# A language-model tower on one core: weights fetched in the first stage, decay attention's folding moved into its ramp, routing weights spread in pairs

## What is computed

```
h = tok(x)                                  # two gathered halves of a row, each projected and gated
h = h + attn(layernorm(h))                  # one head of 64
h = h + block(layernorm(h))                 # rms norm, rotary attention (4 heads), then 8 experts, top 2
    hh = silu(flat @ w1[e].T) * (flat @ w3[e].T);  out += weights[:, e] * (hh @ w2[e].T)
h = h + decay(layernorm(h))                 # causal filter of 5 taps, layer norm, attention of 8 heads
    p_ = softmax(scores);  dist = sqrt((total - cumsum(p_)) * pos);  scores *= exp(-softplus(gamma) * dist)
h = h + mlp(layernorm(h))                   # routed: the 63 best tokens of a sequence go through gelu MLP
```

## Time and profile before

| | us |
|---|---|
| median of three runs | 2688.34 |
| lowest and highest | 2672.03, 2693.78 |
| profiled execution, its own time | 2694.7 |
| its span in the profile | 2692.7 |
| PE busy | 2431.4 (90%) |
| DVE busy | 1908.5 (71%) |
| ACT busy | 1464.7 (54%) |
| POOL busy | 1203.3 (45%) |
| bytes moved by DMA, mean rate | 21.31 MB, 8 GB/s |

### The profile page before, as it was taken

How to read it: one execution, slowest core, us unless ns; L and a number is a source line. 1 busy time by engine, 2 the same in 40 slices (tenths; PEclk the granted TensorE clock), 3 DMA queues, 4 the chain that set the end, 5 groups by cost and what they waited for, 6 DMA issues and landing times. The chain is left out here.

```text
span 2692.7 us, 57001 instructions
## 1 busy us (share of the span) xinstructions
PE 2431.4 (90%) x20912; PEld 1545.5 (57%) x20912; DVE 1908.5 (71%) x4056; ACT 1464.7 (54%) x2886; POOL 1203.3 (45%) x1544
## 2 busy tenths in 40 slices
PE   6999859999959999999999659999999999999485
PEld 5988736777742222222222147777777777776364
DVE  4589637777746666666666558999899999986524
ACT  1234326666643333333333237888888898886332
POOL 6356114444420000000000037888788888875361
PEclk9999759999979999999999868999899999996677
DMA  2111000000000000000000000000000000000003
GB/s 46 24 36 39 8 8 2 2 2 2 2 19 1 1 1 1 1 1 1 1 1 1 23 1 2 2 2 2 2 2 2 2 2 2 2 2 2 5 1 63
DMA packets 31477, 21.31 MB, mean 8 GB/s; under 512 B 24537, under 2 KB 28761, under 8 KB 31220
## 3 DMA queue, kind: packets, MB, share of 16 engines
q0 software_dynamic: 6144, 9.84, 1.6%
q1 hardware_dynamic: 25076, 8.03, 1.3%
HBM read 13.66 MB, written 4.19 MB: 7 GB/s over the span
## 5 line engine op out<-in xcount | busy, mean ns | idle before, releaser
L1123 ACT ACTIVATE act<-c_h 128x512 f32<-128x512 f32 x352 | 210.2, 597 | 407.1 <-PE c_h L1054 407.1
L1210 DVE TENSOR_TENSOR hid<-c_wb,prod 128x512 f32<-128x512 f32 x352 | 243.0, 690 | 241.6 <-PE c_wb L1063 233.0
L1054 PE MATMUL c_h<-flatT,e_w 64*128 64x512 f32 x704 | 398.5, 646 | 10.5 <-DVE owner L1200 10.4
L1055 PE MATMUL c_h<-flatT,e_w 64*128 64x512 f32 x704 | 398.5, 646 | 0.0
L1026 POOL TENSOR_TENSOR H<-H,c_turned 128x256 f32<-128x256 f32 x32 | 23.4, 731 | 691.1 <-ACT c_turned L1117 691.1
L1362 POOL TENSOR_TENSOR d_decay<-d_later,d_posg 128x768 f32<-128x768 f32 x128 | 233.4, 1824 | 48.4 <-DVE d_later L1752 48.3
L1218 DVE TENSOR_TENSOR prod<-c_h,act 128x512 f32<-128x512 f32 x352 | 239.4, 680 | 0.2
L1752 DVE TENSOR_TENSOR_SCAN d_later<-d_cont,d_S 128x384 f32<-128x384 f32 x256 | 229.3, 937 | 1.6 <-ACT d_S L1669 1.6
L1054 PEld LDWEIGHTS c_h<-flatT,e_w 64*128 64x128 f32 x704 | 104.4, 186 | 181.1 <-ACT act L1123 133.4
L1073 PE MATMUL c_out<-hid,e_w 128*64 128x512 f32 x704 | 206.7, 617 | 0.1
L1063 PEld LDWEIGHTS c_wb<-wT,owner 24*128 24x128 bf16 x352 | 31.9, 91 | 267.9 <-issue 169.8
(11 more groups left out here) (348 smaller groups left out, 6060.4 us busy)
## 6 DMA issues: line engine op xcount, KB each, us to landing
out_h<-g_Y SPq DMA_DIRECT2D x8, 512.0 KB, 4.0
rows<-in_table,idx POOLq DMA_INDIRECT x128
e_w<-in_e_w SPq DMA_DIRECT2D x1, 704.0 KB
e_w<-in_e_w SPq DMA_DIRECT2D x1, 352.0 KB
d_conv<-in_d_conv SPq DMA_DIRECT2D x1, 320.0 KB
d_wqk<-in_d_wqk SPq DMA_DIRECT2D x1, 256.0 KB
d_pos<-in_d_pos SPq DMA_DIRECT2D x1, 192.0 KB
d_cont<-in_d_cont SPq DMA_DIRECT2D x1, 192.0 KB
```

The lines of the kernel that those rows point to most:

```text
L1054: nc.tensor.matmul(b1[u][:], w13[0:D, cols], flatT[0:D, x], start=True, stop=True).then_inc(h1_made, 1)
L1055: nc.tensor.matmul(b3[u][:], w13[D:P, cols], flatT[D:P, x], start=True, stop=True).then_inc(h3_made, 1)
L1123: nc.scalar.activation(act1[q % 2][:], b1[q % 2][:], ACT.Silu).then_inc(activated, 1)
L1210: nc.vector.tensor_tensor(hid[q % KEEP_HID][:], bw[u][:], prod[u][:], ALU.mult).then_inc(weighted, 1)
```

## The change

Four edits go together.

1. All weight tiles are allocated once (`early_constants`), and SP issues the 51 loads of the four later stages right behind the 11 of the embedding stage (`load_early`), with one semaphore a stage. The later stages have no SP program of their own for loads; DVE, PE and ACT wait for the same counts as before (the expert stage for 6 in place of 5, because `owner` is fetched twice).
2. The decay stage clears four small tiles, and its loop starts at once. The folding is cut up: convolution at K = -14, projections (with the constants of v) at -11, decay rates and mask at -8, positions in four slices at -7 to -4, the carried bias at -1. Each user waits for the semaphore of its part: PE at its first filter, its first projection and its first scores, ACT at its first copy of v, POOL at its first use of the positions. The instruction mix is the same.
3. The routing weights stand twice in `wts`, now bf16 and padded to 2 x 32 columns, so that the turned `wT` has 24 rows at partitions 0 and 24 at partition 32, and so has `owner`. `spread` runs at even steps only and makes the weights of two chunks, one from each strip, into the two banks. Its wait is for both banks (`weighted >= q`). The turning is a bf16 matmul with an identity in place of an fp32 transpose; the spare columns are cleared by POOL.
4. Routing runs on eighths of the sequences (`QUARTERS = NG // 4`) with one step at every chunk (`PACE` 1, was 3); the first eighth is ahead of everything.

```diff
 phase_embed_attend, sync
+                load_early(sp, dram, T, early)
 phase_block_attention
-            @block.sync
-            def _(sp):
-                for dst, name in ((wq, "f_wq"), (wk, "f_wk"), (wkp, "f_wkp"), (wv, "f_wv"), (wo, "f_wo"),
-                                  (ln1, "f_ln1"), (ln2, "f_ln2"), (router, "router")):
-                    for half in range(2):
-                        sp.dma_start(dst[half * D:(half + 1) * D, :], dram[name]).then_inc(loaded, 16)
...
 phase_experts
-    QUARTERS = NG // 8
+    QUARTERS = NG // 4
...
-    ROUTE, PACE = 25, 3
+    ROUTE, PACE = 25, 1
...
-        wts = m.sb("wts", [P, NB, PARTS, NE])
+        wts = m.sb("wts", [P, NB, 2, STRIP], BF16)
...
+                pool.memset(wts[:, :, :, SPAN:], 0.0).then_inc(spare, 1)
...
-                        last = nc.tensor.transpose(bt[0:PARTS * NE, b * P:(b + 1) * P],
-                                                   wts[:, n * GB + b].rearrange("p k e -> p (k e)"), ident[:])
+                        last = nc.tensor.matmul(bt[0:2 * STRIP, b * P:(b + 1) * P],
+                                                wts[:, n * GB + b].rearrange("p k e -> p (k e)"), ident_b[:],
+                                                start=True, stop=True)
...
                 def spread(q):
-                    n, c, u = q // NCH, q % NCH, q % 2
-                    if c == 0:
-                        pe.wait_ge(wT_kept, n + 1)
+                    pe.wait_ge(wT_kept, (q + 1) // NCH + 1)
                     if q >= 2:
-                        pe.wait_ge(weighted, q - 1)
-                    nc.tensor.matmul(bw[u][:], owner[:, c * P:(c + 1) * P], wT[n % 2][:], start=True, stop=True)\
-                        .then_inc(wb_made, 1)
+                        pe.wait_ge(weighted, q)
+                    for side in range(2):
+                        n, c = (q + side) // NCH, (q + side) % NCH
+                        rows = slice(side * STRIP, side * STRIP + SPAN)
+                        nc.tensor.matmul(bw[side][:], owner[rows, c * P:(c + 1) * P], wT[n % 2][rows, :],
+                                         start=True, stop=True).then_inc(wb_made, 1)
...
-                    if t < LAST:
+                    if t < LAST and t % 2 == 0:
                         spread(t)
...
+                nc.vector.tensor_copy(ident_b[:], ident[:]).then_inc(ready, 1)
                 nc.vector.tensor_scalar(w13[:], w13[:], ln2[:, 0:1], None, ALU.mult).then_inc(ready, 1)
-                nc.vector.tensor_copy(owner[:], owner_f[:]).then_inc(ready, 1)
+                for side in range(2):
+                    rows = slice(side * STRIP, side * STRIP + SPAN)
+                    nc.vector.tensor_copy(owner[rows, :], owner_f[rows, :]).then_inc(ready, 1)
 phase_decay_attention
+        PREPARE_CONV, PREPARE_PROJ, PREPARE_SOFT = FIRST_STEP + 2, FIRST_STEP + 5, FIRST_STEP + 8
...
+                        if m + 1 == 0:
+                            pe.wait_ge(carried, 1)
+                            nc.tensor.matmul(bT[:, 0:D], bv_wide[:], wout[:, 0:D], start=True, stop=True)\
+                                .then_inc(folded, 1)
+                            pe.wait_ge(proj_ready, PROJ_READY)
...
+                def spread_positions(pair):
+                    heads = slice(2 * pair, 2 * pair + 2)
+                    nc.vector.tensor_tensor(posg[:, heads], pos[:, None, :].to_broadcast([P, 2, SEG]),
+                                            over(gam[:, heads], SEG), ALU.mult).then_inc(soft_ready, 1)
...
                 for K in range(FIRST, LAST + 1):
                     m, j = K // PAIRS, K % PAIRS
+                    if K == PREPARE_CONV:
+                        prepare_convolution()
+                    if K == PREPARE_PROJ:
+                        prepare_projections()
+                    if K == PREPARE_SOFT:
+                        prepare_softmax()
+                    if PREPARE_SOFT < K <= PREPARE_SOFT + PAIRS:
+                        spread_positions(K - PREPARE_SOFT - 1)
+                    if K == -1:
+                        carry_bias()
+                        dve.wait_ge(soft_ready, SOFT_READY)
...
+def load_early(sp, dram, T, loaded):
+    for name in ("f_wq", "f_wk", "f_wkp", "f_wv", "f_wo", "f_ln1", "f_ln2", "router"):
+        for half in range(2):
+            sp.dma_start(T[name][half * D:(half + 1) * D, :], dram[name]).then_inc(loaded["block"], 16)
+    for name in ("rope_q", "cos_k", "sin_k", "hide"):
+        sp.dma_start(T[name][:], dram[name]).then_inc(loaded["block"], 16)
+    for name in ("rank", "e_ln2", "e_w13"):
+        sp.dma_start(T[name][:], dram[name]).then_inc(loaded["experts"], 16)
...
```

More of the change, by code:

```diff
@@ L970, in phase_experts @@
     PARTS = 3
+    SPAN = PARTS * NE
+    STRIP = 32
     NG = NB // GB
@@ L1731, in _ @@
-                for u in range(2):
-                    nc.vector.memset(later[u][:, 0:1], 0.0).then_inc(chain, 1)
-                for u in range(KEEP_V):
-                    nc.vector.memset(v[u][:, :, :, HD:HD + 1], 1.0).then_inc(chain, 1)
-                    nc.vector.memset(v[u][:, :, :, HD + 1:], 0.0).then_inc(chain, 1)
-                steps[0] += 2 + 2 * KEEP_V
-                dve.wait_ge(chain, steps[0])
-                nc.vector.memset(xT[:, :, 0:PADT], 0.0).then_inc(ready, 1)
-                nc.vector.memset(rstd[:], 0.0).then_inc(ready, 1)
@@ new lines, in load_early @@
+def load_early(sp, dram, T, loaded):
[6 more added lines that the diff above has]
+        sp.dma_start(T[name][:], dram[name]).then_inc(loaded["experts"], 16)
+    for side in range(2):
+        rows = slice(side * 32, side * 32 + dram["owner"].shape[0])
+        sp.dma_start(T["owner"][rows, :], dram["owner"]).then_inc(loaded["experts"], 16)
+    sp.dma_start(T["e_w2"][:], dram["e_w2"].rearrange("(c p) n -> p c n", p=P)).then_inc(loaded["experts"], 16)
+    for name in ("d_wqk", "d_wv", "d_wout", "d_conv", "d_beta", "d_convb", "d_lnw", "d_lnb", "d_bqk", "d_bv", "d_outb",
+                 "d_gam", "d_pos", "d_cont", "d_hide", "d_notfirst", "d_half"):
+        sp.dma_start(T[name][:], dram[name]).then_inc(loaded["decay"], 16)
+    sp.dma_start(T["d_diag"][:], dram["ident"]).then_inc(loaded["decay"], 16)
+    for half in range(2):
+        sp.dma_start(T["g_w1"][half * D:(half + 1) * D, :], dram["g_w1"]).then_inc(loaded["mlp"], 16)
+    for name in ("g_b1", "g_b2", "g_wr", "g_br"):
+        sp.dma_start(T[name][:], dram[name]).then_inc(loaded["mlp"], 16)
+    sp.dma_start(T["g_w2"][:], dram["g_w2"].rearrange("(c p) n -> p c n", p=P)).then_inc(loaded["mlp"], 16)
@@ L2124, in tower @@
         ident = m.sb("ident", [P, P])
+        T = early_constants(m, dram)
         const_loaded = m.sem("const_loaded")
+        early = {stage: m.sem(f"early_{stage}") for stage in ("block", "experts", "decay", "mlp")}
         with nc.Block() as block:
```

259 lines of the change are left out of this document (133 added, 126 removed).

## The result

The changed kernel takes 2565.74 us (median of 4, 2562.83 to 2578.17), the one before, measured beside it, 2689.55 us (2672.03 to 2693.78): a ratio of 0.957, 95% interval 0.952 to 0.962. Medians and ratios in this document leave out executions that took over 1.5% longer than the fastest of the same kernel. The profiled execution has a span of 2561.1 us against 2692.7. Direction and mechanism came as forecast; the gain is larger than the sum of -95.3 us.

The account below looks back on a forecast made before the run. PE was taken to bound the expert stage, no single engine the decay stage, with idle stretches between stages. Terms -53 - 3 - 6.7 - 14.0 - 5.4 - 15.2 + 2 = -95.3 us gave 2593 us, range 2570 to 2619.

Parts of the forecast that it names:

- Pairs, -53: Expert stage: two spreading matmuls run side by side in one slot, 176 x 0.30 = 53 us less, PE still the bound.
- (a): Rival, expert stage: the spreading pair does not overlap, -17.6 in place of -53, 2628 us; chance 0.10.
- (d): Rival, expert stage: PE stalls at each pair waiting for DVE's hid, slower than before, 2725 us at 0.75 us a stall; chance 0.02.
- stage of about 656 us: Sign, expert stage: PE at 99% or more of a stage of this length, period of two chunks 3.44 us.
- Turning, -3: Expert stage: 32 times four fp32 transposes become bf16 matmuls, 7 us in all, cut to 3 for weight loads between them.
- Routing head, -6.7: Start of expert stage: load wait -5.0, extra casts +0.9, routing steps on half the elements -2.6 us.
- Block loads, -14.0: Start of block stage: DVE's wait for small DMAs, 357.0 to 371.10 us, goes whole, 14.0 us.
- Decay, -15.2: Decay stage start: no load wait, folding partly hidden in the ramp, 15.2 us less; bounds -10.1 and -30.3.
- Last stage, -5.4: Start of last stage: DVE's load wait of 5.40 us goes.
- Embedding, +2: Embedding stage: early loads contend with row gathers for the DMA engines, 2 us more; bounds 0 and 14.7 us.
- rival (c): Decay stage: PE's mean clock differs by execution, 2583 or 2603 us; inside the forecast's range, no chance of its own.
- (b): Rival: gathers collide with loads in the embedding stage (+12.7) and the decay ramp hides no folding (+5.1), 2611 us; chance 0.09.

Follow-up runs that it names:

- x_old_experts: Changed kernel with the expert stage of before (single spreading, fp32 turning, routing in quarters), weights still loaded early: 2666.5 us, expert stage 734.8 us.
- x_late_loads: Changed kernel with each later stage's weights again fetched at that stage's own start: 2632.6 us median, ratio 0.974 to the kernel before.
- x_after_64: Changed kernel with the spreading pair on rows 0 to 63 and 64 to 127, eight turning matmuls a group: 2540.5 us median, ratio 0.941 to the kernel before.
- x_before_64: Kernel before with its single spreading matmul widened by rows of zeros to 64 rows: 2619.0 us, expert stage 679.1 us.
- the first four experiments: Changed kernel with late loads (2632.6 us), folding ahead of the ramp (2583.8 to 2654.7), old expert stage (2666.5), or both pair matmuls on the same rows (2607.5).
- x_64_back: Changed kernel with pairs on 64-row strips and output matmuls ahead of the products at odd visits: 2564.3 us median beside 2585.2 of the changed kernel.
- r_after: Changed kernel profiled once more, unchanged, beside the kernel before on the same chip: span 2583.4 us.

## Why the prediction was right, and where it was not

- **Pairs, -53.** Right in the mechanism: they start together, DVE's wait is hidden, PE stays the bound; rivals (a) and (d) are refuted by the pair's one slot of 0.31 us and by 623 busy us in 627. The size was off: the stage came out at 657.9 us, where the sum gives 739.7 - 62.7 = 677.0. (The "stage of about 656 us" among the signs is the window of 713 us less 57, not this stage; that it is near 657.9 is chance.) The failed step is the slot of a pair costed alone ("176 x 0.30"): the prediction saw the 0.10 us for a change of kind, but put it only at the spreading matmul itself. The product passes on both sides of a visit pay it too, 0.53 against 0.43 us. Where the visit goes and products meet products, 0.20 more is saved, 66 times by count of the order: 13.2 us.
- **Turning, -3.** It takes 0.32 us (0.54 before), not 0.45: 32 x 0.22 = 7.0 us. I had taken weight loads to stand between the four; the slot leaves no room for them. These two make 17 of the 19 us by which the stage beat its forecast; 2 are not assigned.
- **Routing head, -6.7.** As measured. Each part fits: casts and folding end at 754.07, 5.3 us after the start, and a routing step lasts 0.29 us. The loads' share is 4.9 by the stage with all else old (x_old_experts); late in the new stage they cost 7.8 (x_late_loads).
- **Block loads, -14.0.** The wait of 14.09 us is gone; the stage gained 16.7, and 15.9 by x_late_loads. The prediction counted the wait alone. What the other 2 to 3 us are no run tells apart: they are within the spread of one profile (412.8 to 416.9 us with the same code), though the means of eight and four profiles differ by 16.5; and the record shows 50 us of the lower clock in that stage after, 73 before.
- **Decay, -15.2.** -15.6 at the first scores. Late loads bring them back by 11.4, folding ahead of the ramp by 5.9 us: both parts near the 10.1 and 5.1 of the working. From the first scores to the stage's end the same code took 909.9 to 924.4 us in seven profiles, the code of before 915.0 to 921.4 in three: no effect there beside the clock. Against the second and third profile of the old code (58.1 and 58.2) the scores came 16.8 and 16.9 us earlier.
- **Last stage, -5.4.** The second table load comes 30.0 us after the start, 35.6 before: -5.5. But the stage is 8.0 us longer, so 13.5 were lost behind that point. It goes with the clock: with the same code the stage lasts 184.7 us with 89 us of lower clock in it, 189 with 97 and 200 with 118. The profile after has 21.6 us more of the lower level there than the one before, half of which is 10.8; the other 2.7 stay open. Step wrong: none in the term; that the saving would survive in one execution's stage length.
- **Embedding, +2.** PE's waits for rows, which answer to the earlier trace rows, and PE at the same place of both kernels later, after and then before:

```profile
33.92 0.49 PE L249 MATMUL a_rows_T<-ident,rows 128*75 128x128 f32 x1 [2.35 <-DMA rows<-in_table,idx]
45.51 0.63 PE L249 MATMUL a_rows_T<-ident,rows 128*75 128x128 f32 x2
```
```profile
42.63 0.63 PE L248 MATMUL a_rows_T<-ident,rows 128*75 128x128 f32 x2
```

Contention cost 2.9 us (42.63 to 45.51), and it stays at 2.9 until 73 us. The other profiles without the pause of the last section agree: this row comes at 42.62 to 42.66 in the three without early loads and at 45.45 to 45.95 in the three with them. That is far from the bound of 14.7 us for gathers that stand behind all loads. The stage nevertheless ended 23.3 us earlier, because of the clock. Two windows of before, then of after:

```profile
60.00:100.00 40.00, 40.00 (x167) 34.98 (x167) 22.03 (x83) 9.63 (x26) 17.34 (x24) 1.00 0.13 30
100.00:140.00 40.00, 40.00 (x175) 36.09 (x174) 20.70 (x77) 10.34 (x27) 14.32 (x21) 1.00 0.10 23
```
```profile
60.00:100.00 40.00, 39.88 (x227) 35.90 (x227) 25.38 (x95) 12.59 (x37) 18.51 (x26) 1.00 0.13 30
100.00:140.00 40.00, 38.94 (x315) 35.18 (x314) 38.10 (x145) 17.07 (x48) 26.41 (x39) 1.00 0.18 42
```

Before, PE is busy all of both windows and gets through 175 instructions in the second; after, 315 in as much time. The column shows 1.00 in all four, but there is no record ahead of the first rise, at 150.0 us before and at 85.6 us after, and the pace of the instructions tells the level. The cause is not the loads: without them the rise came at 83.4, 85.3, 145.2 and 150.0 us, with them at 73.6, 85.6, 86.1, 94.2, 96.2, 99.0, 161.6 and 188.5. Nor is the rise all: with the same code the stage took 333.7 us with 67 us of lower level recorded in it, and 359.1 with 98 (some 9 of the difference of 25 lie in a pause that the last section tells of). Both together tell the length. Add the time up to the rise and the lower level recorded behind it, and take half of that off the stage: 253.6 to 257.5 us are left in the six profiles without the pause, 261.3 to 270.9 in the six with it, where the stages themselves last 326.5 to 427.0. Between the first two profiles this half differs by 27.0 us, beside the 26.2 (23.3 and 2.9) to be explained. Why PE, busy in all the windows read ahead of the rise, is given the upper level at such different moments stays open.

So rival (c), the clock, was named but in the wrong stage and with too small a size: 10 us in the decay stage, where the first stage varied from 326.5 to 427.0 us over twelve profiles. The spread of 0.8% over three times, from which the prediction took what can be told from no change, was small by luck: later executions of the kernel before spread over 42 to 200 us in a session. With what is put down to the clock taken off (-26.2 in the first stage, +13.5 in the last, -2.2 in the decay stage), the profiles differ by 116.7 us, against 95.3 forecast. In the last stage that is in part a remainder and not measured. The difference of 21 us is 19 in the expert stage, 2.7 in the block stage and 0.4 in the decay stage's ramp, less 0.9 of contention and with 0.1 of the last stage's loads. So of the 36 us by which the profiles passed the forecast some 15 are the clock's and 21 the kernel's own.

Two small slips of the prediction: the chances of the forecast, (a) and (b) add up to 0.97, not 0.96; and in the 8 us at 789 not all stands, DVE is busy 2.95 us and ACT 3.43. Neither changes the sum.

## What to carry to other kernels

Before pricing a matmul that stands between others, write down which rows and columns each takes, and count the changes of grouping on both sides of it: a short matmul of 0.21 us cost 0.31 in its own slot and 0.20 at its neighbours, and padding it with zeros to their grouping gave three quarters of the stage's gain with no pairing at all. Then look again at the engine that hands over: where PE's own time shrank further, ACT's activation and copies began to hold it up. Prefer a pair in the neighbours' grouping to a pair in smaller strips. Compare two profiles by their stages and by moments inside them, not by their ends: here the stages that nobody had sped up moved the end by more than most of the edits.

## What the runs showed of the hardware that was not expected

- A change of row grouping between matmuls cost 0.09 us (22.4 / 240, x_after_64) to 0.13 us (60.7 / 481, x_before_64) where it was taken out, and 0.18 us to and from the output matmuls where it was left; a change between bf16 and f32 in the same grouping costs nothing that can be seen (0.21 us from start to start, x_before_64).
- A bf16 spreading matmul on 64 rows starts together with an f32 product pass on the other 64 rows (1165.96 us in x_before_64).
- TensorE first rose to the upper level at 73.6 to 188.5 us from the start, in kernels with the same first stage for PE; before the rise it was busy all of the 40 us of a window (60 to 100 and 100 to 140 us in the kernel before).
- In the profiles of two sessions (the first four experiments, x_64_back and r_after), with early loads or without, ACT and DVE stand until 40 to 45 us, released by something that the trace puts down as remote, and PE pauses with them for 9 to 11 us, until 42 to 46 us. The other six profiles, of both kernels, have no such gap. What it is stays open. One such row of x_late_loads, where it can't be the early loads:

```profile
45.17 0.69 DVE L448 COPY rowsT<-a_rows_T 75x512 f32<-75x512 f32 x1 [9.40 <-remote]
```
